# Two mixtures of experts on rows sorted by expert, in three parts of the tokens

## The reference

```
p = softmax(x[t] @ router_weight)          # 8 experts
for the two largest p[e]:
    g, u = split(x[t] @ w1[e], 2)          # 128 -> 2 x 176
    y += p[e] * ((silu(g) * u) @ w2[e])    # 176 -> 128
x[t] = normalise(x[t] + y)
```

```
g   = argmax softmax(x[t] @ w_group + b_group)                 # 4 groups
e   = argmax softmax(x[t] @ w_expert[g] + b_expert[g])         # 2 experts of the group
y   = p_group * p_expert * (relu(x[t] @ w1[e] + b1[e]) @ w2[e] + b2[e])   # 128 -> 256 -> 128
```

## Time and profile before

| | |
|---|---|
| time of the kernel, median of 3 runs | 4686.77 us (4686.62 to 4692.56) |
| the profiled execution's own time | 4658.31 us |
| its span, first to last instruction | 4656.5 us |
| PE busy | 3992.7 us, 86% |
| DVE busy | 3324.2 us, 71% |
| ACT busy | 2208.0 us, 47% |
| POOL busy | 1392.6 us, 30% |
| first mixture, from its first DMA to the first DMA of the next stage | 718.2 to 1324.3 us |
| second mixture, likewise | 2588.0 to 2931.8 us |

### The profile page before, as it was taken

One profiled execution on the slowest core, in us unless ns is written; L12 is line 12 of the kernel. 1 busy time (PEld: TensorE's weight loads), 2 busy tenths in 40 slices (PEclk: granted clock), 3 DMA queues, 4 the chain that ended last, 5 costly groups with the idle time before them and its releaser, 6 DMA issues. The chain is left out here.

```text
span 4656.5 us, 142989 instructions
## 1 busy us (share of the span) xinstructions
PE 3992.7 (86%) x51849; PEld 2927.6 (63%) x51890; DVE 3324.2 (71%) x7831; ACT 2208.0 (47%) x3967; POOL 1392.6 (30%) x2469
## 2 busy tenths in 40 slices
PE   8997997999989999889899561799998968879986
PEld 6775666565667877767677441577675434447765
DVE  7986883555557777678788316788786767759985
ACT  4554552222224344356588133455784345545543
POOL 5653341000000000012245505233222234435543
PEclk9998996999999999999999585899998978889998
DMA  2011111000000000011000252000111200000001
GB/s 72 27 46 36 38 36 35 11 14 10 10 13 1 0 0 0 1 41 44 29 17 17 66 149 63 12 13 13 32 33 43 57 7 0 0 12 23 23 17 36
DMA packets 184580, 127.91 MB, mean 27 GB/s; under 512 B 43056, under 2 KB 175408, under 8 KB 184112
## 3 DMA queue, kind: packets, MB, share of 16 engines
q1 hardware_dynamic: 168128, 110.62, 8.0%
q0 software_dynamic: 4096, 8.40, 0.6%
q10 hardware_dynamic: 12144, 6.03, 0.4%
HBM read 77.24 MB, written 18.35 MB: 21 GB/s over the span
## 5 line engine op out<-in xcount | busy, mean ns | idle before, releaser
L920 DVE TENSOR_TENSOR L0f_SG<-L0f_SG,L0f_psY 128x512 f32<-128x512 f32 x176 | 120.6, 685 | 219.5 <-PE L0f_psY L849 219.0
L888 ACT ACTIVATE L0f_SG<-L0f_psY 128x512 f32<-128x512 f32 x176 | 105.1, 597 | 357.1 <-PE L0f_psY L847 357.1
L860 PEld LDWEIGHTS L0f_psO<-L0f_W,L0f_G 128*128 128x128 f32 x1408 | 182.2, 191 | 101.5 <-issue 61.9
L860 PE MATMUL L0f_psO<-L0f_W,L0f_G 128*128 128x128 f32 x1408 | 188.3, 277 | 17.1 <-DVE L0f_G L924 10.9
L2351 POOL TENSOR_TENSOR L1a_rs<-L1a_ag,eps 128x1 f32<-128x1 f32 x64 | 12.1, 189 | 593.9 <-DVE L1a_ag L2521 593.9
L847 PE MATMUL L0f_psY<-L0f_XT,L0f_W 128*128 128x512 f32 x352 | 182.1, 599 | 0.7 <-ACT L0f_G3T L876 0.7
L849 PE MATMUL L0f_psY<-L0f_XT,L0f_W 128*128 128x512 f32 x352 | 180.6, 595 | 2.3 <-issue 0.2
L1531 POOL TENSOR_TENSOR L0f_rt<-L0f_ag,eps 128x4 f32<-128x4 f32 x16 | 3.2, 200 | 513.5 <-DVE L0f_ag L1525 513.5
L2461 ACT ACTIVATE L1a_PR<-L1a_PR 128x1024 f32<-128x1024 f32 x64 | 67.6, 1056 | 150.5 <-DVE L1a_PR L2482 150.5
L2443 PE MATMUL L1a_psO<-L1a_WO,L1a_OT 128*128 128x128 f32 x1024 | 133.7, 285 | 2.9 <-DVE L1a_OT L2497 2.6
L2443 PEld LDWEIGHTS L1a_psO<-L1a_WO,L1a_OT 128*128 128x128 f32 x1024 | 122.3, 196 | 20.0 <-issue 16.8
(11 more groups left out here) (647 smaller groups left out, 12914.8 us busy)
## 6 DMA issues: line engine op xcount, KB each, us to landing
L1m_WB<-in_w12b SPq DMA_DIRECT2D x23, 321.0 KB, 3.3
L1m_BUF<-sorted_x SPq DMA_DIRECT2D x23, 256.0 KB, 3.6
sorted_y<-L1m_BUF ACTq DMA_DIRECT2D x23, 256.0 KB, 3.8
L0a_CS<-in_ctx SPq DMA_DIRECT2D x32, 128.0 KB, 2.1
KB<-L0a_KT SPq DMA_DIRECT2D x128, 32.0 KB, 1.8
L0x_CS<-in_ctx SPq DMA_DIRECT2D x32, 128.0 KB, 2.1
L0x_CR<-in_ctxT SPq DMA_DIRECT2D x32, 128.0 KB, 2.3
KB<-L0x_KT SPq DMA_DIRECT2D x128, 32.0 KB, 1.8
```

Of the source, the lines that this page charges most:

```text
L860: m = nc.tensor.matmul(psO[:, j, :], G[:, gb, 0, j * P:(j + 1) * P], W2[:, k, :], start=k == 0 and j == 0, stop=k == NCH - 1, skip_group_c ...
L888: nc.scalar.activation(SG[:, yb, :], psY[:, yb, 0, :], ACT.Silu).then_inc(S["silu"].sem, 1)
L920: nc.vector.tensor_tensor(SG[:, yb, :], SG[:, yb, :], psY[:, yb, 1, :], ALU.mult).then_inc(S["product"].sem, 1)
```

## The change

Both mixtures now use one function, `routed_experts(L, top, weights, router, bias, XO)`; `moe` and `packed_experts` are gone. The tokens are cut into three parts of 16, 24 and 24 tiles. Each part has its own `sorted_x`, `sorted_y` and table of blocks. The number of blocks of a part is fixed: as many as the worst split over eight experts needs, (top x tokens - 8) // 512 + 8. With top = 2 these are 15 + 19 + 19 = 53 blocks, with top = 1 they are 11 + 13 + 13 = 37.

```diff
+                    for p in parts:
+                        made(sp, "prep", p + 1)
+                        for e in range(NE):
+                            last = sp.value_load(BT[0:1, p, 2, e:e + 1], min_val=0, max_val=ROWS - BATCH)
+                            sp.dma_start(rows_at(sorted_x[p], last), AC2[:, 0]).then_inc(S["stored"].sem, 16)
+                    made(sp, "stored", 16 * len(PARTS) * (SPARE + NE))
...
+                    def rows(J):
+                        p = part_of[J]
+                        if J == first[p]:
+                            made(sp, f"scattered{p}", 16 * top * PARTS[p])
...
+                        made(sp, "turned2", J - 3)
+                        sp.dma_start(XB[:, J % 4], rows_at(sorted_x[p], start)).then_inc(S[ROWS_IN[J % 4]].sem, 16)
...
+                        made(sp, "expert" if gated else "expert_out", J - 3)
+                        sp.dma_start(WB[:, J % 4, :], io[weights][bass.ds(which, P), :]).then_inc(S[WEIGHTS_IN[J % 4]].sem, 16)
...
+                    for J in range(3):
+                        expert(J)
+                    for J in range(3):
+                        rows(J)
+                    for J in range(BLOCKS):
+                        if J + 3 < BLOCKS:
+                            if part_of[J + 3] == part_of[J]:
+                                rows(J + 3)
+                            expert(J + 3)
+                        if J + 1 < BLOCKS and part_of[J + 1] != part_of[J]:
+                            for k in range(J + 1, J + 4):
+                                rows(k)
+                        if gated and J < NBATCH:
+                            side_rows(J)
```

```diff
+                    for p in parts:
+                        for t in range(part_tile[p], part_tile[p + 1]):
+                            if t % GT == 0:
+                                made(g, "scanned", t // GT + 1)
+                            for k in range(top):
+                                nc.gpsimd.indirect_dma_start(out=sorted_x[p][:, :], ...
...
+                    for p in parts:
+                        made(g, "cut", p + 1)
+                        for n in range(3):
+                            made(g, STORED[n], 16 * len(range(n, first[p + 1], 3)))
+                        for b in range(lo, hi):
+                            made(g, "mix", b - 3)
+                            for t in range(b * TB, (b + 1) * TB):
+                                for k in range(top):
+                                    nc.gpsimd.indirect_dma_start(out=YG[:, b % 4, k, t % TB, :], ...
+                            if gated and b - 1 >= lo:
+                                root(b - 1)
```

```diff
+                        if gated:
+                            made(pe, "silu", 2 * (J - 1) + 1)
+                            nc.tensor.matmul(psH[:, 0, :], WB[:, J % 4, 0:P], XT[:, J % 2, :], ...
+                            made(pe, "g_ready", 2 * (J - 1) + 1)
+                            nc.tensor.matmul(psH[:, 1, :], WB[:, J % 4, P:2 * P], XT[:, J % 2, :], ...
+                            made(pe, "g_ready", 2 * J)
+                            nc.tensor.matmul(psH[0:112, 2, :], WB[:, J % 4, 2 * P:2 * P + 112], XT[:, J % 2, :], ...
```

```diff
+                    for J in range(BLOCKS):
+                        if gated:
+                            for c, f, at in CHUNKS:
+                                made(dv, "silu", 2 * J + c + 1)
+                                made(dv, ("hidden2", "hidden")[c], (J + 1, 2 * J + 2)[c])
+                                made(dv, "expert", J - 1)
...
+                                nc.vector.tensor_tensor(G[0:f, J % 2, c, :], SG[0:f, c, :], up, ALU.mult).then_inc(S["g_ready"].sem, 1)
+                            if J < NBATCH:
+                                side_work(J)
+                        else:
+                            made(dv, "expert", J + 1)
...
+                            nc.vector.tensor_tensor(YB[:, J % 3], psO[:, J % 2], ...
+                        if J in step_after:
+                            (tail_pair if gated else tail_one)(step_after[J])
+                    for b in range(done_steps, STEPS):
+                        (tail_pair if gated else tail_one)(b)
```

More of the change, by code:

```diff
@@ L1004, in _ @@
[L1004 to L1015 removed]
+                    n = 3 if gated else 4
@@ L1127, in _, with out_and_store @@
[L1127 to L1130 removed]
+                        made(act, "hidden", 2 * (J - 1))
+                        nc.scalar.activation(XT[:, J % 2, :], psX[:, J % 2, :], ACT.Copy).then_inc(S["xt_out"].sem, 1)
+                    def out_and_store(J):
+                        if OUT_ON_ACT:
+                            made(act, "expert", J + 1)
+                            made(act, STORED[J % 3], 16 * (J // 3))
+                            nc.scalar.activation(YB[:, J % 3], psO[:, J % 2], ACT.Copy).then_inc(S["expert_out"].sem, 1)
+                        made(act, "expert_out", J + 1)
+                        nc.scalar.dma_start(rows_at(sorted_y[part_of[J]], (J - first[part_of[J]]) * BATCH), YB[:, J % 3]).then_inc(S[STORED[J % 3]].sem, 16)
@@ new lines, in _ @@
+                    rows(0)
+                    for J in range(BLOCKS):
+                        if J + 1 < BLOCKS and part_of[J + 1] == part_of[J]:
+                            rows(J + 1)
+                        for c in range(2):
+                            made(act, "hidden", 2 * J + c + 1)
+                            if gated:
+                                f = (P, 48)[c]
+                                made(act, "g_ready", 2 * J + c - 1)
+                                nc.scalar.activation(SG[0:f, c, :], psH[0:f, 2 * c, :], ACT.Silu).then_inc(S["silu"].sem, 1)
+                            else:
+                                made(act, "expert", J - 1)
+                                nc.scalar.activation(G[:, J % 2, c, :], psH[:, c, :], ACT.Relu, bias=WB[:, J % 4, 512 + c:513 + c]).then_inc(S["g_ready"].sem, 1)
+                        if J and part_of[J - 1] == part_of[J]:
+                            out_and_store(J - 1)
+                        if J + 1 == BLOCKS or part_of[J + 1] != part_of[J]:
+                            out_and_store(J)
+                            if J + 1 < BLOCKS:
+                                rows(J + 1)
+                        if J in step_after and step_after[J]:
+                            tail(step_after[J] - 1)
@@ L1146, in _ @@
+                    for b in range(done_steps - 1, STEPS):
+                        tail(b)
                 @block.vector
@@ L1187, in place @@
+                        link(nc.vector.reciprocal(gate[:, 0, tiles], MG[:, 2, :]))
                     def place(g_):
+                        p = max(q for q in parts if part_tile[q] <= g_ * GT)
+                        opening, closing = g_ * GT == part_tile[p], (g_ + 1) * GT == part_tile[p + 1]
+                        before = base8 if opening else carry[:, g_, :]
                         made(dv, "gates_out", g_ + 1)
-                        got = psR[:, 0:(GT + 1) * NE].rearrange("p (t e) -> p t e", e=NE)
```

826 lines of the change are left out of this document (301 added, 525 removed).

## The result

| | before | after |
|---|---|---|
| median of the timed runs, same chip | 4686.69 us | 4796.28 us (4788.89 to 4800.2) |
| ratio, 95% interval | | 1.023 (1.0217 to 1.0243) |
| span of the profiled execution | 4656.5 us | 4798.4 us |
| first mixture | 606.1 us | 677.0 us |
| second mixture | 343.8 us | 408.9 us |

Predicted were 4540 us and faster; the kernel became 2.3% slower. These are the stretches of the changed kernel: sorting, blocks and tail (the last fetches and closing steps) of the first mixture, then of the second. The columns are those of the earlier trace rows.

A forecast was written before the change was run, and what follows sets the result against it. First mixture bound by PE running eight experts where two are wanted, second by a chain of sorting, scattering, blocks and closing. Gains 137 + 15 - 5 = 147 us took 4658.3 to 4511; 28.5 carried over gave 4540, range 4475 to 4640.

The forecast's parts named there:

- Sorting: First mixture, before the blocks: groups of two batches at 7.3 us each, third table at 802.0; bounds 780 to 820.
- the 28.5 us "carried over": Whole kernel: timed median stands 28.5 us above the profiled execution, added unchanged to 4511 to give 4540 us.
- Sort and start: First mixture up to the blocks: third table at 802.0, then zero writes, landing, weights and rows; first turn at 823.5.
- The step "PE's pace is 4.8 us": First mixture's blocks: the second mixture's 3.96 us plus 0.88 for one more first product, 4.8 us a block.
- The rest of the blocks: First mixture's blocks: first 16 at 5.8 from DMA load, other 37 at 4.8, two boundaries 5 each, cold start 3.
- Tail: End of first mixture: only part 2's six batches exposed, set by POOL's fetches, from 1106.9 to 1187.0.
- Second mixture: First turn at 2687.9, blocks 179.5 us, closing 49.3; end 2916.7 against 2931.8 before, gain 15 us.
- Cold clock behind the first mixture: Stage after the first mixture: PE idles 80 us before it, so 5 us lost (0 to 8).
- Late data: Rival, blocks of both mixtures: SP's queue doesn't keep ahead and PE starves; 4667 us, half of it 4604; chance 0.28.
- The POOL chain rival: Both mixtures: indirect DMAs take twice as long beside DVE and other DMAs; 4770 us; chance 0.09 including similar stalls.
- the sort takes over 110 us before the first turn: Sign of being wrong, at the sort before the blocks: over 110 us until the first turn.
- the other two: Signs of being wrong: PE's releaser in the blocks is a DMA all through; POOL's spacing grows when DVE is busy.

The follow-up runs named there:

- e9: The changed kernel, unedited, timed again in a faster series: 4590.15 against 4654.26 us for the kernel before, 0.9863.
- e11: The kernel before, unedited, traced in a slower series: 4683.13 us in one run, its second mixture 370.6 us instead of 343.8.
- e4: Changed kernel with second products ordered by height, two height changes a block: 4768.17 us, 1.0173 of the kernel before.
- e12: Changed kernel with the first mixture's 48-row second products made 128 rows high by zeros: 4768.44 against 4681.16 us, 1.0173.
- e18: Changed kernel with full-height products, blocks running through part ends, waits after every four indirect DMAs, later first-mixture closing steps: 4574.67 against 4682.7 us, 0.9764.
- e20: e18 with DVE's side work of a batch done one block later: 4577.1 against 4676.18 us, 0.9787.
- e1: Changed kernel with POOL waiting for landing after every eight scatters, both mixtures: 4756.33 against 4687.95 us, 1.0139.
- e17: Changed kernel with POOL waiting for the landing of each tile's scatters before the next tile: 4764.18 us in one run.
- e19: Changed kernel with full-height second products and blocks running through part ends, without added waits: 4733.7 against 4682.7 us, 1.0102.

## Why the prediction was wrong

There were two errors in the sum of the changed kernel's time, and one in its starting point. The first alone turned the sign.

**The step "Sorting", and all steps beside scatters.** This step failed. It took 0.25 us for a small instruction and PE's own pace, from a trace in which nothing crawled, and put the effect of POOL's scatters on the other engines at nothing. In the changed kernel's profile the third table is at 886.8, not 802.0, and the first turn at 932.8, not 823.5. Against e9 crawling adds 677.0 - 539.1 = 137.9 us in the first mixture, 118 of them in the sort and 20 in the blocks, and 408.9 - 332.3 = 76.6 in the second, 38 of them in the sort. With what lies around the mixtures the spans differ by 4798.4 - 4579.3 = 219. To the kernel before it adds 27. Two traces with crawling agree with the timed difference of 110 us (4796.28 - 4686.69): 677.0 - 605.7 = 71.3 and 408.9 - 370.6 = 38.3. Without crawling the same change gains 64. The change exposes the kernel to it by sending 384 indirect DMAs instead of 128, 192 of them beside the sorts and blocks that the time hangs on.

**The starting point: the 28.5 us "carried over".** I took the gap between profile and median for one of measuring. It was the one sign, in the numbers of before, that the profile was taken without crawling and the timed runs with it: the 27 us of e11 fit this gap. Followed up, it would not have given the size for the changed kernel, but it said that some 27 us of the kernel before's time stood in no row of its trace.

The rest is judged on e9, where it can be seen alone.

- *Sort and start.* The third table comes after 76.1 us (predicted 83.8), the first turn after 96.9 (105.3): 8 us too dear. In the second mixture the first turn comes after 90.5 (99.9).
- *The step "PE's pace is 4.8 us".* This is the term that failed there: it measured 6.3. The extra first product was right (0.88 predicted, 0.86 measured), but I took the second products from the earlier trace rows, where all have one height; 53 x 1.5 = 79.5 us. e4 and e12 show that it is the change of height. The Trainium skill, TensorEngine Tiling (Array Packing) (section "Tiling Modes"), says that a change of tiling mode drains TensorE. It prices none and does not say that a 48-row product is another mode; the runs agree with it as far as they go, 3.23 us with a change at every product, 2.07 with two a block, 1.78 with none.
- *The rest of the blocks.* The two boundaries take 9 and 4 us (5 each predicted). Over PE's pace the first 16 blocks take about 10 us more (16 predicted, from the DMA share). That this is near is luck: there DVE waits for the side rows that SP queued behind weights and rows (70.0 us in 15 waits), at a DMA share of 0.71. With PE's pace as I had it, these blocks take 7.5 us each (e18) and not the 5.8 predicted, and 5.1 once the wait is mostly gone (e20), so neither the 5.8 nor its reason held. The blocks together take 363.7 us against 283.4.
- *Tail.* It takes 78.5 us, where 80.1 were predicted. POOL sets it, as predicted.
- *Second mixture.* The blocks take 187.3 us (179.5 predicted) at 3.94 us each (3.96), with 7 for a boundary (5), and closing 54.5 (49.3). The gain is 11.5 us instead of 15.
- *Cold clock behind the first mixture.* The next stage takes 664.9 against 664.5 us: nothing, not 5.

So without crawling 147 us were predicted, and 77 came by the spans and 64 by the medians (e9's profiled execution, 4581.11, was its fastest of four). Of the missing 147 - 77 = 70 us PE's longer blocks account for 80 by the sum; the other terms together err by 10 the other way. What the kernel gains when the height is mended was measured only with crawling, where it was 28 us.

**The rivals.** Late data did not come: without crawling PE runs its blocks at clock 0.95. The POOL chain rival had the side right (4770) by luck, for its mechanism was wrong: the indirect DMAs took 957/962/1225 ns, as before the change, and the fetches' tail was on time. What the Trainium skill says of the shared port, named in the prediction, shows in no run here. Its 0.09 with "another stall of that size" is what the outcome had. Of my own signs of being wrong, "the sort takes over 110 us before the first turn" came true, at 214.5; the other two did not: PE waited 51.5 us for rows, of which 49.9 are the start itself, and POOL's spacing did not grow.

**Open.** Why the engines crawl beside indirect DMAs in some series and not in others, and whether that belongs to the chip or to its condition at the time, is not known; no run could look behind the semaphore events. What is shown is that the spacing of the scatters matters in the slower series: at 1.27 us the core crawls, at 1.45 (e1) less, at 1.85 (e18) and 2.28 (e17) hardly or not at all. That increments pile up and cause the ticks was my guess, and the missing records are no proof of it. Whether the recording of events plays a part in the crawling was not tested. e12 to e20 were not measured without crawling, so how far e18 would gain there is not known. The 159 us between e18 and e19 belong to the waits and the later closing steps together; the two were not tried one by one.

## What to carry to other kernels

When a profile and the timed runs differ by more than they scatter, ask which part of the kernel the profile doesn't show, before resting a sum on it. When a result contradicts its explanation, run the unedited kernel again beside the edited one; here that alone showed that the semaphore numbers had changed nothing. That each engine has room does not make a stream of indirect DMAs beside other work free: try it with few in flight (a wait after every four, with later closing steps, gave back more than it cost), and see that what is queued behind them can stand the longer chain. Take the price of a product from a row of the same shape in the same order; a height that alternates from product to product made these almost twice as dear, and here zero rows were cheaper than skipping them.

## What was not expected of the hardware

- One kernel has two times, by the series: the kernel before takes 4654 us in two and 4676 to 4688 in the others, the changed one 4590 in one and 4796 in another.
- After 9 or 10 indirect DMAs 1.265 us apart the other engines advance in ticks of some 0.7 us, in the slower series; POOL itself is not slowed. In the changed kernel's trace many semaphore updates of all engines are missing while it scatters (147 of 251 recorded), and none of 8760 in the stages without indirect DMAs.
- Sixteen passes of 128 columns took 1.78 us at one height and 3.23 us at two alternating ones, 0.11 and 0.20 us each.
